# The last output stream mixed by TensorE, gelu's low part on GpSimd, and another order of units in a gated attention and stream-mixing kernel

## The chip, the cores and the metric

The kernel runs on one core of a Trainium2 chip. The metric is the device time of one execution in microseconds (us), lower is better.

## What is computed

The input x is (8, 512, 2048): eight batches of 512 rows, 2048 columns. Two blocks follow each other, each with a residual:

```
x = x + tanh(g_xattn) * xattn(layernorm(x), ctx, mask, Wq, Wk, Wv, Wo, biases)
x = x + tanh(g_ffn)   * ffn(layernorm(x), W_res, W_pre, W_post, bases, gate, W_branch)
```

xattn cuts the 2048 columns into windows of 128 and does attention inside each: q and k are projections (256 x 512) of the normalised x, v one of ctx, 8 heads of 32, the mask adds a large negative number to masked keys, and the result goes through gelu, then Wo, bias and mask. ffn sees each of the 512 rows as 4 streams of 512. From the row's logits come a 4 x 4 matrix H_res (50 Sinkhorn iterations), H_pre and H_post (softmax over 4):

```
x_pre = einsum('btnc,btn->btc', x_streams, H_pre);  y = x_pre @ W_branch
out_i = sum_j H_res[i,j] * x_j  +  H_post[i] * y          (i, j: streams)
```

## The kernel before

The program is a table of steps g, and every engine walks the same table in its own instruction order. A step with 0 <= g < 256 is a **unit**: one window of 128 columns and 4 of the 8 heads. G = g // 8 is a **chunk** (512 columns of a batch, 32 chunks), r = g % 8 the place in it. Steps from -16 to -1 are the lead-in, steps from 256 on only finish the second block.

In a step TensorE does, in this order, the scores of unit g (L688), the transposed scores of g-1 (L700, L702), values and denominators of g-2 (L715, L719), and then what `banked_at(g)` lists: projections q (r 0, 1), k (r 2, 3) and v (r 6, 7) of the next chunk, the output projection o of the chunk before (two tiles at r 4, two at r 5), transposes and logits of the chunk two before. Each such group fills one of four PSUM banks used in rotation (`RING`), and waits until the group four places earlier has been read (`bank_free`, L571). VectorE takes the row maximum (`maximum`, L998; unit g+1's scores wait for it, since there is one bank for scores), the low bf16 parts of q and k (`low_qk`), `divide` (L1005), the low part of gelu's output (`low_gelu`, L1023, r 3), `read_wo` (r 5, 6), the statistics and a mask row (`mask_row`, L991, r 4, once per chunk). ScalarE does exp, ln, gelu and the high bf16 parts; GpSimd normalises x (`norm_x`) and makes the low parts of x and ctx (`split_x`, `split_ctx`).

The second block of batch f hangs on steps 32(f+1) + e. Its Sinkhorn iterations take 26 steps (`SINK`), two iterations each, that is four halves per step: VectorE reduces and inverts (L1134, L1135), GpSimd multiplies the 4 x 4 matrices by the result (`scale`, L526), VectorE reduces the product, and so on, with other work of the step put between the halves. After that come four **tiles** of 128 rows, eight steps apart, the first at e = 52 (`TILE_AT`). With k the step counted from a tile's own:

- k = -4: ScalarE's first product of x_pre (L876); k = -3: VectorE adds three more (`make_xpre`, L1167)
- k = -1: TensorE transposes x_pre (L675), ScalarE copies it (L884); k = 0: TensorE's `branch`, 4 fp32 matmuls 128x512 (8 instructions, L728)
- k = -1 and 2: ScalarE starts the four output streams, two by two (`first_out`, L893)
- k = 0, 1, 2: VectorE adds x_1, x_2, x_3 to streams 0 and 1 (`add_stream`, L1179, two instructions a step); k = 3: adds y to all four (`add_y`, L1192); k = 4, 6, 7: x_1 to x_3 to streams 2 and 3
- GpSimd stores streams 0 and 1 at k = 4 and 2 and 3 at k = 8 (`store`, L480). The tile of the next group is started only when the pair of the tile before has been stored (`out_stored`).

SyncE issues the loads: x, ctx, masks, statistics pieces, the x1 tiles, and 12 + 12 copies per chunk that stack q and k (L390), in its own fixed order. Besides these it stores x1 (r 0) and copies the mask row under k.

Of the kernel before, what the change touches and what calls it, by code (L numbers as in the profile page):

```python
# [11 lines left out]
P = 128  # L12
B, D, S = 8, 512, 2048
W = 128
# [54 lines left out]
TILE_AT = [52 + UPC * t for t in range(DT)]  # L69
# [36 lines left out]
def stat_steps(b):  # L106

    if b == 1:
        return [1 + p for p in range(XS)]
    last = UNITS * (b - 1) + 16  # L110
    return [last - UPC * (3 - p // 4) - (p % 4 == 0) for p in range(XS)]
# [8 lines left out]
def banked_at(g):  # L120

    G, r = chunk_step(g)
    made = [("t", H, j) for H, j in at_step(g, 2, T_AT)]
    made += [("lg", H, 0) for H, j in at_step(g, 2, [LOGITS_AT])]
    made += [("sel", f, 0) for f in ffn_at(g, UPC + SELECT_AT)]
    made += [("pre", f, t) for f, t in tiles_at(g, -1)]
    if 0 <= G + 1 < NG:
        made += {0: [("q", G + 1, 0)], 1: [("q", G + 1, 1)], 2: [("k", G + 1, 0)], 3: [("k", G + 1, 1)],
                 6: [("v", G + 1, 0)], 7: [("v", G + 1, 1)]}.get(r, [])
    if 0 <= G - 1 < NG and r in (4, 5):  # L130
        made += [("o", G - 1, 2 * (r - 4)), ("o", G - 1, 2 * (r - 4) + 1)]
    if g == -1:
        made.append(("csum", 0, 0))
    return made
# [25 lines left out]
def program(nc, x, ctx4, mask_bc, mask_t, gates, wq_t, bq, wk_t, bk, wv_t, bv, wo_t, bo, wf_t, base,  # L160
            w_branch, ident, stack_i, eye4, out):
    with ExitStack() as ctx:  # L162
# [28 lines left out]
        neg_row = sb("neg_row", [1, CH], BF16)  # L191
        maskt = sb("maskt", [P, 2, S // W])
        key_bias = sb("key_bias", [P, 2, S // W])
# [52 lines left out]

        pool_ps = [ps(f"pr{i}") for i in range(RING)]
# [19 lines left out]
        maskt_loaded = [sem(f"maskt_loaded{i}") for i in range(2)]  # L267
# [52 lines left out]
        xpre_ready = sem("xpre_ready")  # L320
        y_full = sem("y_full")
# [32 lines left out]
        def _(sp):  # L354
# [10 lines left out]
            def load_maskt(b):  # L365
                sp.dma_start(maskt[:, b % 2, :], mask_t[b]).then_inc(maskt_loaded[b % 2], 16)

# [40 lines left out]
            load_maskt(0)  # L408
# [3 lines left out]
            load_maskt(1)  # L412
# [3 lines left out]
            for g in range(FIRST, LAST):  # L416
# [5 lines left out]
                if r == 0 and 0 <= G - 2 < NG:  # L422
                    store_x1(G - 2)
# [7 lines left out]
                if r == 5 and 0 <= G + 1 < NG:  # L431
                    sp.wait_ge(qk_ready, 4 * (G + 1) + 4)
                    stack(G + 1, k_st, ((k_hl, 0), (k_hl, 0), (k_hl, 1)))
                    sp.wait_ge(negrow_ready, G + 2)
                    sp.dma_start(k_st[ROWS:ROWS + 1, (G + 1) % 2].rearrange("p t h j -> p (t h) j"),
                                 bcast(neg_row[:], 1, HEADS)).then_inc(stack_loaded[(G + 1) % 2], 16)
# [7 lines left out]
                if u == UPC + 6 and g >= 0 and b + 2 < B:  # L444
                    sp.wait_ge(bias_ready, b + 1)
                    load_maskt(b + 2)

        @block.gpsimd
        def _(pool):
# [13 lines left out]
            def split_ctx(G, t):  # L463
                pool.wait_ge(ctx_hi, DT * G + t + 1)
                ins = nc.gpsimd.tensor_tensor(ctx_hl[:, 1, t, :], ctx_raw[:, t, :], ctx_hl[:, 0, t, :], ALU.subtract)  # L465
                if t == DT - 1:
                    ins.then_inc(ctx_split, 1)

# [68 lines left out]
            for g in range(FIRST, LAST):  # L537
# [20 lines left out]
                if 0 <= G - 1 < NG and r in (6, 7):  # L558
                    add_x(G - 1, r - 6)
                for done, t in tiles_at(g, 4):  # L560
                    store(done, t, 0)
                for done, t in tiles_at(g, 8):
# [5 lines left out]
        def _(pe):  # L568
            PARTS = ((0, 0), (0, 1), (1, 0))

            def bank_free(what):  # L571
# [105 lines left out]

            def scores(k):
# [53 lines left out]
            for g in range(FIRST, LAST):  # L732
# [6 lines left out]
                for what in banked_at(g):  # L739
# [13 lines left out]
                    elif what[0] == "pre":  # L753
                        transpose_pre(what)
                    else:
# [5 lines left out]
        def _(act):  # L761
# [36 lines left out]
            def exp_scores(k):  # L798
                b, w = divmod(k // ET, S // W)
                if k % UNITS == 0:  # L800
                    act.wait_ge(bias_ready, b + 1)
                act.wait_ge(st_full, k + 1)
                if k >= 2:
                    act.wait_ge(av_full, k - 1)
                nc.scalar.activation(probs[:, k % 2, :], st_ps[:], ACT.Exp,  # L805
                                     bias=key_bias[:, b % 2, w:w + 1], scale=SCALE).then_inc(exp_done, 1)
# [79 lines left out]
            def first_out(f, t, pair):  # L886
                n = DT * f + t
                if t == 0 and pair == 0:
                    act.wait_ge(coef_ready, 2 * f + 2)
                if n:  # L890
                    act.wait_ge(out_stored[pair], 16 * n)
                for i in range(2 * pair, 2 * pair + 2):
                    nc.scalar.activation(otile[:, i, :], x1t[n % 2][:, 0:C], ACT.Identity,  # L893
                                         bias=ccon[:, f % 2, t, i:i + 1],
                                         scale=cmat[:, f % 2, t, i, 0:1]).then_inc(acc_ready, 1)
# [16 lines left out]
            for g in range(FIRST, LAST):  # L912
# [8 lines left out]
                for what in banked_at(g):  # L921
# [8 lines left out]
                    elif what[0] == "pre":  # L930
                        copy_pre(what)
                for H, t in at_step(g, -1, HI_CTX_AT):
# [3 lines left out]
                if g == FIRST + UPC + 3:  # L936
# [7 lines left out]
                for done, t in tiles_at(g, -4):  # L944
                    first_products(done, t)
                for done, t in tiles_at(g, -1):
                    first_out(done, t, 0)
                for done, t in tiles_at(g, 2):
                    first_out(done, t, 1)
# [11 lines left out]
        def _(dve):  # L961
# [3 lines left out]
            def stat_piece(b, p):  # L965
                q = XS * b + p
                dve.wait_ge(xs_loaded[q % XSN], 16 * (q // XSN + 1))
                nc.vector.bn_stats(bn_a[:, p // 4, p % 4, :], xs[:, q % XSN, :]).then_inc(xs_taken, 1)
# [17 lines left out]
            def bias_row(b):  # L986
                dve.wait_ge(maskt_loaded[b % 2], 16 * (b // 2 + 1))
                nc.vector.tensor_scalar(key_bias[:, b % 2, :], maskt[:, b % 2, :], 0.0, NEG * SCALE,
                                        ALU.is_le, ALU.mult).then_inc(bias_ready, 1)

            def mask_row(G):  # L991
                dve.wait_ge(mask_loaded[G % NC], 16 * (G // NC + 1))
                if G:
                    dve.wait_ge(stack_loaded[(G - 1) % 2], STACKED * ((G - 1) // 2 + 1))
                nc.vector.tensor_scalar(neg_row[:], maskbc[0:1, G % NC, :], 0.0, NEG, ALU.is_le, ALU.mult
# [26 lines left out]

            def low_gelu(G, et):  # L1023
                n = ET * G + et
                dve.wait_ge(gelu_hi, n + 1)
                nc.vector.tensor_tensor(o_part(G, et, 1), g_sb[:, et, :], o_part(G, et, 0), ALU.subtract
                                        ).then_inc(gelu_done, 1)
# [146 lines left out]
            def add_stream(f, t, pair, j):  # L1174
                x1 = x1t[(DT * f + t) % 2]
                for i in range(2 * pair, 2 * pair + 2):
                    if j == 1 and pair == 0:
                        dve.wait_ge(acc_ready, (DT * f + t) * N + i + 1)
                    ins = nc.vector.scalar_tensor_tensor(out=otile[:, i, :], in0=x1[:, j * C:(j + 1) * C],  # L1179
                                                         scalar=cmat[:, f % 2, t, i, j:j + 1], in1=otile[:, i, :],  # L1180
                                                         op0=ALU.mult, op1=ALU.add)
                if pair and j == N - 1:
# [4 lines left out]
            def add_y(f, t):  # L1187
                dve.wait_ge(y_full, DT * f + t + 1)
                for i in range(N):
# [5 lines left out]
                    if i == 1:  # L1195
                        ins.then_inc(out_ready, 1)
# [23 lines left out]
            for g in range(FIRST, LAST):  # L1220
# [101 lines left out]
```

## Time and profile before

| | |
|---|---|
| runs | median 1905.74 us (1904.44 to 1910.57, 3 runs) |
| the profiled execution | 1909.33 us, of which the span is 1907.5 us |
| VectorE busy | 1439.4 us, 75% |
| TensorE busy (matmul) | 1392.2 us, 73% |
| ScalarE busy | 945.7 us, 50% |
| GpSimd busy | 863.2 us, 45% |
| TensorE's mean granted clock | 0.884 of full |

Times are counted from the first instruction. L numbers are lines of the kernel before. "Busy" sums instruction times; idle time is put down to what ended it. Matmuls overlap, so TensorE's busy time is somewhat above the time it really needs.

### The profile page before, as it was taken

Reading aid. Unit: us, or ns where it says so; the run is one execution under the profiler, and the core shown is the slowest. Engines: PE = TensorE matmul, PEld = TensorE weight load, DVE = VectorE, ACT = ScalarE, POOL = GpSimd, SP = SyncE. Lnnn points to the kernel's source line nnn. Section 1 sums busy time; section 2 is a strip of 40 time slices with the busy share of each in tenths; the row PEclk is TensorE's granted clock in tenths of the full one; section 3 lists DMA queues with packets and bytes.
Section 4 is the critical chain, followed back from the end, with each engine's and each line's share of the span. In section 5 each row is a group of like instructions: output and inputs, shape, how many; then the busy total and the mean of one; then the engine's idle time right before and its main releaser. Section 6 shows DMA issues by size and latency. Waiting matters only on the chain. (4 is left out here: it accounts for less than half of the span.)

```text
span 1907.5 us, 35318 instructions
## 1 busy us (share of the span) xinstructions
PE 1392.2 (73%) x12301; PEld 849.8 (45%) x12448; DVE 1439.4 (75%) x3684; ACT 945.7 (50%) x1889; POOL 863.2 (45%) x1461
## 2 busy tenths in 40 slices
PE   2788999888888787888888887878788875511323
PEld 0555556555544454445544554445455553200111
DVE  3344556767788888888888888888888888777787
ACT  2455676564655555554655555555555454210112
POOL 3433334555455545455465645554555523323310
PEclk9898999998999999998999999989999987755556
DMA  7456676566666665666666566665555543321123
GB/s 245 135 149 191 195 195 163 166 170 179 171 184 179 181 178 160 177 185 181 182 174 184 163 192 167 192 171 147 169 165 166 144 120 91 88 77 44 56 96 113
DMA packets 173984, 299.79 MB, mean 157 GB/s; under 512 B 23664, under 2 KB 74736, under 8 KB 169712
## 3 DMA queue, kind: packets, MB, share of 16 engines
q1 hardware_dynamic: 147184, 230.41, 39.2%
q0 software_dynamic: 26624, 67.12, 15.3%
q8 instruction: 100, 1.64, 0.4%
q14 instruction: 76, 0.62, 0.1%
HBM read 179.75 MB, written 67.11 MB: 129 GB/s over the span
## 5 line engine op out<-in xcount | busy, mean ns | idle before, releaser
L1134 DVE TENSOR_REDUCE ssum<-kp 128x16 f32<-128x64 f32 x768 | 181.7, 237 | 175.7 <-POOL kp L526 170.5
L526 POOL TENSOR_TENSOR kp<-ke,sv 128x64 f32<-128x64 f32 x376 | 183.9, 489 | 277.2 <-DVE sv L1135 274.4
L526 POOL TENSOR_TENSOR kp<-ke,sa 128x64 f32<-128x64 f32 x392 | 126.8, 323 | 329.1 <-DVE sa L1135 329.1
L805 ACT ACTIVATE probs<-st_ps,key_bias 128x512 f32<-128x512 f32 x256 | 174.5, 682 | 199.7 <-PE st_ps L702 193.9
L604 PE MATMUL pr<-x_hl,wk 128*128 128x512 bf16 x736 | 195.7, 422 | 66.0 <-DVE k_hl L982 65.2
L1002 DVE TENSOR_REDUCE negm<-s_ps 128x4 bf16<-128x512 f32 x256 | 167.7, 655 | 75.6 <-PE s_ps L688 73.0
L604 PE MATMUL pr<-x_hl,wq 128*128 128x512 bf16 x707 | 192.2, 420 | 44.5 <-POOL x_hl L460 38.3
L460 POOL TENSOR_TENSOR x_hl<-xc,x_hl 128x512 bf16<-128x512 f32 x128 | 157.4, 1230 | 136.9 <-ACT x_hl L773 136.5
L618 PE MATMUL pr<-wv,ctx_hl 128*128 128x256 bf16 x1536 | 188.6, 282 | 23.4 <-POOL ctx_hl L465 23.4
L465 POOL TENSOR_TENSOR ctx_hl<-ctx_raw,ctx_hl 128x512 bf16<-128x512 f32 x128 | 176.5, 1379 | 59.1 <-ACT ctx_hl L767 59.1
L688 PE MATMUL s_ps<-k_st,q_st 97*128 97x128 bf16 x1024 | 102.4, 223 | 111.4 <-DVE negm L1002 98.2
L631 PE MATMUL pr<-o_sb,wo 128*128 128x512 bf16 x714 | 176.6, 385 | 4.4 <-issue 1.5
L618 PEld LDWEIGHTS pr<-wv,ctx_hl 128*128 128x128 bf16 x1536 | 151.4, 102 | 56.7 <-issue 35.6
L688 PEld LDWEIGHTS s_ps<-k_st,q_st 97*128 97x128 bf16 x1024 | 73.6, 99 | 188.8 <-DVE negm L1002 123.0
L700 PE MATMUL st_ps<-q_st,k_st 96*128 96x128 bf16 x1024 | 149.8, 223 | 7.3 <-ACT probs L805 4.4
L604 PEld LDWEIGHTS pr<-x_hl,wk 128*128 128x128 bf16 x768 | 79.6, 106 | 160.1 <-DVE k_hl L982 64.1
L702 PE MATMUL st_ps<-id_bf,negm 128*128 128x128 bf16 x1024 | 149.3, 223 | 0.0
L1010 DVE TENSOR_TENSOR o_sb<-av_ps,rden 128x128 f32<-128x128 f32 x256 | 70.4, 275 | 104.3 <-ACT rden L814 103.9
L715 PE MATMUL av_ps<-probs,v_t 128*32 128x128 f32 x2048 | 112.2, 291 | 42.8 <-DVE o_sb L1010 42.4
L728 PE MATMUL f<-wb,xpt 128*128 128x512 f32 x256 | 135.8, 680 | 8.5 <-ACT xpt L884 8.5
L604 PEld LDWEIGHTS pr<-x_hl,wq 128*128 128x128 bf16 x768 | 76.2, 106 | 145.7 <-issue 46.9
L675 PE MATMUL pr<-id_sb,xpre 128*128 128x128 f32 x128 | 24.0, 320 | 160.2 <-DVE xpre L1167 160.2
(140 smaller groups left out, 3079.2 us busy)
## 6 DMA issues: line engine op xcount, KB each, us to landing
xs<-in_dram SPq DMA_DIRECT2D x128, 256.0 KB, 3.9
xc<-in_dram SPq DMA_DIRECT2D x32, 1024.0 KB, 5.9
ctx_raw<-in_dram SPq DMA_DIRECT2D x32, 1024.0 KB, 5.1
x1c<-in_dram POOLq DMA_DIRECT2D x64, 512.0 KB, 6.0
x_dram<-x1c SPq DMA_DIRECT2D x32, 1024.0 KB, 5.4
out_dram<-otile POOLq DMA_DIRECT2D x64, 512.0 KB, 3.5
q_st<-q_hl SPq DMA_DIRECT2D x384, 64.0 KB
k_st<-k_hl SPq DMA_DIRECT2D x384, 64.0 KB
```

Of the source, the lines that this page charges most:

```text
L460: nc.gpsimd.tensor_tensor(x_hl[:, G % 2, 1, t, :], xc[:, t, :], x_hl[:, G % 2, 0, t, :], ALU.subtract).then_inc(x_split, 1)
L465: ins = nc.gpsimd.tensor_tensor(ctx_hl[:, 1, t, :], ctx_raw[:, t, :], ctx_hl[:, 0, t, :], ALU.subtract)
L526: nc.gpsimd.tensor_tensor(kp[:], ke[:], v, ALU.mult).then_inc(kp_made, 1)
L604: ins = nc.tensor.matmul(bank(what)[:], w[:, a, t, i * P:(i + 1) * P], x_hl[:, G % 2, m, t, :], start=(t == 0 and a + m == 0), stop=(t == ...
L618: ins = nc.tensor.matmul(bank(what)[:, j * E:(j + 1) * E], ctx_hl[:, a, t, win], wv[:, m, t, :], start=(t == 0 and a + m == 0), stop=(t == ...
L631: ins = nc.tensor.matmul(bank(what)[:], wo[:, a, et, t * P:(t + 1) * P], o_part(G, et, m), start=(et == 0 and a + m == 0), stop=(et == ET ...
L688: ins = nc.tensor.matmul(s_ps[:, h * W:(h + 1) * W], q_st[0:ROWS + 1, G % 2, et, h, win], k_st[0:ROWS + 1, G % 2, et, h, win], start=True, ...
L700: nc.tensor.matmul(part, k_st[0:ROWS, G % 2, et, h, win], q_st[0:ROWS, G % 2, et, h, win], start=True, stop=False)
L702: ins = nc.tensor.matmul(part, negm[:, k % 2, h:h + 1].broadcast_to([P, P]), id_bf[:], start=False, stop=True)
L805: nc.scalar.activation(probs[:, k % 2, :], st_ps[:], ACT.Exp, bias=key_bias[:, b % 2, w:w + 1], scale=SCALE).then_inc(exp_done, 1)
L1002: nc.vector.tensor_reduce(negm[:, k % 2, :], s_ps[:].rearrange("p (h j) -> p h j", h=HPT), AX.X, ALU.max, negate=True).then_inc(max_done, 1)
L1134: cf.link(nc.vector.tensor_reduce(s_t, k, AX.X, ALU.add))
```

## The change

1. **The last stream goes to TensorE.** Stream 3 of a tile is sum_j H[3,j] x_j. GpSimd makes four 128x128 diagonal matrices from the coefficients (`make_diag`, k = -1); TensorE multiplies them with the x1 tile, 4 fp32 matmuls 128x512 into one bank (`mix`, k = 1, behind `branch`); ScalarE writes the bank out with its constant (`copy_mix`, k = 1) in place of its `first_out` for that stream. VectorE's three additions for it go. Stream 2 keeps its three on VectorE, now one behind the other at k = 5.
2. **low_gelu moves from VectorE (r 3) to GpSimd (r 4)**, between parts 0 and 1 of `scale`; `make_diag` stands between parts 2 and 3.
3. **Mask rows and key biases are made once**, in the lead-in, from two loads, in place of one VectorE instruction per chunk and one per batch.
4. **Another order.** Both v groups at r 4 (were r 6, 7), o at r 5 and 6 (were 4, 5), transposes, logits, splits and statistics at other r; tiles start at e = 54; inside a tile: x_pre at k = -2, streams 0 and 1 at k = 1, 3, 4, y at k = 2, stores at k = 5 and 6; add_x h = 1 at r 0 of the next chunk, the x1 store at r 2, the ctx load at r 4.

```diff
-NORM_AT, HI_X_AT, LOW_X_AT = [2, 3, 4, 5], [3, 4, 5, 6], [4, 5, 6, 7]
-HI_CTX_AT, LOW_CTX_AT = [0, 0, 1, 4], [1, 2, 3, 5]
-T_AT, LOGITS_AT, SELECT_AT = [2, 2, 3, 3], 4, 6
-STAT_B_AT = [2, 4]
+NORM_AT, HI_X_AT, LOW_X_AT = [2, 3, 4, 5], [3, 5, 5, 6], [5, 6, 6, 7]
+HI_CTX_AT, LOW_CTX_AT = [-1, 0, 0, 1], [0, 1, 2, 3]
+T_AT, LOGITS_AT, SELECT_AT = [3, 4, 4, 5], 6, 7
+STAT_B_AT = [2, 5]
-TILE_AT = [52 + UPC * t for t in range(DT)]
+TILE_AT = [54 + UPC * t for t in range(DT)]
-    return [last - UPC * (3 - p // 4) - (p % 4 == 0) for p in range(XS)]
+    return [UNITS * (b - 1) + UPC * (p // 4 - 2) + (1, 5, 6, 6)[p % 4] for p in range(XS)]
@@ banked_at @@
+    made += [("mix", f, t) for f, t in tiles_at(g, 1)]
-                 6: [("v", G + 1, 0)], 7: [("v", G + 1, 1)]}.get(r, [])
-    if 0 <= G - 1 < NG and r in (4, 5):
+                 4: [("v", G + 1, 0), ("v", G + 1, 1)]}.get(r, [])
+    if 0 <= G - 1 < NG and r in (5, 6):
@@ sync @@
-            load_maskt(0)
+            sp.dma_start(maskt, mask_t.rearrange("b p n -> p b n")).then_inc(masks_loaded, 16)
+            sp.dma_start(mask_rows, mask_bc.rearrange("b (n j) -> (b n) j", j=CH)).then_inc(masks_loaded, 16)
-                if r == 0 and 0 <= G - 2 < NG:
+                if r == 2 and 0 <= G - 2 < NG:
                     store_x1(G - 2)
-                if r == 6 and 1 <= G + 2 < NG:
+                if r == 4 and 1 <= G + 2 < NG:
                     sp.wait_ge(ctx_split, G + 2)
                     load_ctx(G + 2)
@@ gpsimd @@
+            def low_gelu(G, et):
+                pool.wait_ge(gelu_hi, ET * G + et + 1)
+                nc.gpsimd.tensor_tensor(o_part(G, et, 1), g_sb[:, et, :], o_part(G, et, 0), ALU.subtract
+                                        ).then_inc(gelu_done, 1)
+            def make_diag(f, t):
+                ...
+                for j in range(N):
+                    ins = nc.gpsimd.tensor_scalar(diag[:, j, :], id_sb[:], cmat[:, f % 2, t, N - 1, j:j + 1], None,
+                                                  ALU.mult)
+                ins.then_inc(diag_made, 1)
+                if 0 <= G - 1 < NG and r == 4:
+                    for et in range(ET):
+                        low_gelu(G - 1, et)
+                for ready, t in tiles_at(g, -1):
+                    make_diag(ready, t)
@@ tensor @@
+                elif kind == "mix":
+                    pe.wait_ge(acc_ready, N * (DT * c + i) + 3)
+            def mix(what):
+                ...
+                pe.wait_ge(diag_made, n + 1)
+                for j in range(N):
+                    ins = nc.tensor.matmul(bank(what)[:], diag[:, j, :], x1t[n % 2][:, j * C:(j + 1) * C],
+                                           start=(j == 0), stop=(j == N - 1))
+                ins.then_inc(bank_full, 1)
@@ scalar @@
+            def copy_mix(what):
+                ...
+                act.wait_ge(bank_full, PLACE[what] + 1)
+                if n:
+                    act.wait_ge(out_stored[1], 16 * n)
+                nc.scalar.activation(otile[:, N - 1, :], bank(what)[:], ACT.Identity,
+                                     bias=ccon[:, f % 2, t, N - 1:N]).then_inc(acc_ready, 1)
@@ vector @@
-                if 0 <= G - 1 < NG and r == 3:
-                    for et in range(ET):
-                        low_gelu(G - 1, et)
-                for k, pair, j in ((0, 0, 1), (1, 0, 2), (2, 0, 3), (4, 1, 1), (6, 1, 2), (7, 1, 3)):
+                for k, j in ((1, 1), (3, 2), (4, 3)):
                     for done, t in tiles_at(g, k):
-                        add_stream(done, t, pair, j)
-                for done, t in tiles_at(g, 3):
+                        add_stream(done, t, j, (0, 1))
+                for done, t in tiles_at(g, 2):
                     add_y(done, t)
-                for done, t in tiles_at(g, -3):
+                for done, t in tiles_at(g, 5):
+                    for j in range(1, N):
+                        add_stream(done, t, j, (2,))
+                for done, t in tiles_at(g, -2):
                     make_xpre(done, t)
-                if r == 0 and 0 <= G + 1 < NG and (G + 1) % NC == 0:
-                    bias_row((G + 1) // NC)
-                if r == 4 and 0 <= G + 1 < NG:
-                    mask_row(G + 1)
+                if g == -6:
+                    mask_parts()
```

## Rows read from the trace of the kernel before

**Rows 1.** The page: the span and the engines' busy time, share and instructions

```profile
span 1907.5 us, 35318 instructions
...
PE 1392.2 (73%) x12301; PEld 849.8 (45%) x12448; DVE 1439.4 (75%) x3684; ACT 945.7 (50%) x1889; POOL 863.2 (45%) x1461
```

**Rows 2.** Windows: length, busy PE, PEld, DVE, ACT, POOL (count), clock, DMA share, GB/s

```profile
70.00:388.00 318.00, 280.63 (x2862) 178.95 (x2892) 172.76 (x399) 186.79 (x388) 131.94 (x182) 0.96 0.62 173
...
788.00:1412.00 624.00, 512.01 (x4596) 311.40 (x4656) 529.88 (x1372) 350.83 (x705) 330.55 (x546) 0.94 0.61 174
...
1600.00:1830.00 230.00, 62.74 (x218) 32.52 (x216) 171.52 (x501) 41.74 (x76) 73.19 (x186) 0.58 0.23 73
```

**Rows 3.** Groups by line in 788 to 1412 us: count | busy us, mean ns | idle before

```profile
L1002 DVE TENSOR_REDUCE negm<-s_ps 128x4 bf16<-128x512 f32 x96 | 62.2, 648 | 2.6 <-PE s_ps L688 2.4
```

**Rows 4.** VectorE's waits in 788 to 1412 us: total us, times, longest us

```profile
DVE ssum L1134 <- POOL kp L526: 52.0, 80, 1.6
DVE o_sb L1010 <- ACT rden L814: 21.5, 19, 1.8
```

**Rows 5.** TensorE's waits in 788 to 1412 us

```profile
PE s_ps L688 <- DVE negm L1002: 47.7, 42, 3.0
PE pr L604 <- DVE k_hl L982: 37.6, 12, 3.7
```

**Rows 6.** Timeline of VectorE in one chunk: start, us, instructions, idle before

```profile
904.10 2.32 DVE L1167 SCALAR_TENSOR_TENSOR xpre<-x1t_even,pre,xpre 128x512 f32<-128x512 f32 x3
...
916.17 1.29 DVE L1026 TENSOR_TENSOR o_sb<-g_sb,o_sb 128x512 bf16<-128x512 f32 x2 [0.23 <-ACT o_sb L830]
917.38 1.41 DVE L1179 SCALAR_TENSOR_TENSOR otile<-x1t_odd,cmat,otile 128x512 f32<-128x512 f32 x2
```

**Rows 7.** Groups by line, whole span

```profile
L454 POOL TENSOR_SCALAR xc<-xc,ra 128x512 f32<-128x512 f32 x128 | 106.9, 835 | 9.0 <-DMA xc<-in_dram 7.5 <-POOL ra L500 1.4
...
L787 ACT ACTIVATE q_hl<-pr,bq_sb 128x512 bf16<-128x512 f32 x64 | 43.9, 685 | 140.9 <-PE pr L604 140.9
...
L995 DVE TENSOR_SCALAR neg_row<-maskbc 1x512 bf16<-1x512 f32 x32 | 17.9, 561 | 0.4 <-issue 0.2
...
L507 POOL TENSOR_SCALAR rb<-mv_b 128x4 f32<-128x4 f32 x8 | 1.9, 232 | 0.7
```

**Rows 8.** The instructions of line 460: shortest/median/longest ns

```profile
L460 POOL TENSOR_TENSOR x_hl<-xc,x_hl x128: 1145/1159/2054, 30.9 to 1512.8; 128x512 bf16<-128x512 f32 x128
```

**Rows 9.** Timeline of TensorE in one chunk

```profile
921.95 3.60 PE L728 MATMUL f<-wb,xpt 128*128 128x512 f32 x8
...
931.65 2.78 PE L618 MATMUL pr<-wv,ctx_hl 128*128 128x256 bf16 x24 [0.88 <-POOL ctx_hl L465]
```

**Rows 10.** Timeline of TensorE in the lead-in

```profile
58.67 7.68 PE L618 MATMUL pr<-wv,ctx_hl 128*128 128x256 bf16 x48 [8.26 <-POOL ctx_hl L465]
```

**Rows 11.** The chain that ended last, in the last Sinkhorn steps: start, us

```profile
1706.15 0.30 POOL kp L526
...
1707.02 1.29 DVE otile L1179 x2
```

**Rows 12.** The same chain, last four tiles

```profile
1840.25 7.03 DMA out_dram<-otile
...
1857.15 6.94 DMA out_dram<-otile
...
1864.83 0.81 ACT otile L893
...
1889.56 5.36 PE f L728 x8
...
1895.02 2.74 DVE otile L1192 x4
```

**Rows 13.** Timeline of TensorE, last four tiles

```profile
1839.09 6.68 PE L728 MATMUL f<-wb,xpt 128*128 128x512 f32 x8 [0.69 <-ACT xpt L884]
...
1887.79 1.09 PE L675 MATMUL pr<-id_sb,xpre 128*128 128x128 f32 x4 [9.79 <-DVE xpre L1167]
```

More of the change, by code:

```diff
@@ L266, in program @@
         mask_loaded = [sem(f"mask_loaded{i}") for i in range(NC)]
-        maskt_loaded = [sem(f"maskt_loaded{i}") for i in range(2)]
+        masks_loaded = sem("masks_loaded")
         stack_loaded = [sem(f"stack_loaded{i}") for i in range(2)]
@@ L754, in _ @@
                         transpose_pre(what)
+                    elif what[0] == "mix":
+                        mix(what)
                     else:
@@ L884, in copy_pre, with first_out @@
                 nc.scalar.activation(xpt[:], bank(what)[:], ACT.Copy).then_inc(xt_copied, 1)
-            def first_out(f, t, pair):
+            def first_out(f, t, i):
                 n = DT * f + t
-                if t == 0 and pair == 0:
+                if t == 0 and i == 0:
                     act.wait_ge(coef_ready, 2 * f + 2)
-                if n:
[L891 to L895, printed above, removed]
+                if n and i != 1:
+                    act.wait_ge(out_stored[i // 2], 16 * n)
+                nc.scalar.activation(otile[:, i, :], x1t[n % 2][:, 0:C], ACT.Identity,
+                                     bias=ccon[:, f % 2, t, i:i + 1],
+                                     scale=cmat[:, f % 2, t, i, 0:1]).then_inc(acc_ready, 1)
+            def copy_mix(what):
+                kind, f, t = what
+                n = DT * f + t
+                act.wait_ge(bank_full, PLACE[what] + 1)
+                if n:
+                    act.wait_ge(out_stored[1], 16 * n)
+                nc.scalar.activation(otile[:, N - 1, :], bank(what)[:], ACT.Identity,
+                                     bias=ccon[:, f % 2, t, N - 1:N]).then_inc(acc_ready, 1)
             def w_parts(i, dst, loaded):
@@ L931, in _ @@
                         copy_pre(what)
+                    elif what[0] == "mix":
+                        copy_mix(what)
                 for H, t in at_step(g, -1, HI_CTX_AT):
@@ L943, in _ @@
                     xstat(b + 1)
-                for done, t in tiles_at(g, -4):
+                for done, t in tiles_at(g, -5):
                     first_products(done, t)
[L946 to L949, printed above, removed]
+                for done, t in tiles_at(g, 0):
+                    for i in range(2):
+                        first_out(done, t, i)
+                for done, t in tiles_at(g, 1):
+                    first_out(done, t, 2)
                 for n in range(2):
@@ L967, in stat_piece @@
                 dve.wait_ge(xs_loaded[q % XSN], 16 * (q // XSN + 1))
+                if b and p == 0:
+                    dve.wait_ge(mv_a_ready, b)
                 nc.vector.bn_stats(bn_a[:, p // 4, p % 4, :], xs[:, q % XSN, :]).then_inc(xs_taken, 1)
@@ L1172, in make_xpre, with add_stream @@
                 ins.then_inc(xpre_ready, 1)
[L1174 to L1179, printed above, removed]
+            def add_stream(f, t, j, which):
+                n = DT * f + t
+                for i in which:
+                    if j == 1 and i < 2:
+                        dve.wait_ge(acc_ready, N * n + i + 1)
+                    ins = nc.vector.scalar_tensor_tensor(out=otile[:, i, :], in0=x1t[n % 2][:, j * C:(j + 1) * C],
                                                          scalar=cmat[:, f % 2, t, i, j:j + 1], in1=otile[:, i, :],
                                                          op0=ALU.mult, op1=ALU.add)
-                if pair and j == N - 1:
+                if j == N - 1:
                     ins.then_inc(out_ready, 1)
```

71 lines of the change are left out of this document (33 added, 38 removed).

## The prediction

> **What bounds the kernel now.** I read the page first, for the share of each engine, then windows by stage, then the waits inside the longest stage, and last the chain that ended last. The sum is made against the profiled execution, 1909.3 us with a span of 1907.5 [rows 1]; the median of the runs shown is 3.6 us lower, and I subtract that at the end. About 0.3% (5.7 us) is what a measurement of this kernel can tell from no change.
>
> Four stages need different readings. From 70 to 388 us (the first 64 units) TensorE is busy 281 of 318 us and VectorE only 173 [rows 2]: TensorE sets the pace. From 788 to 1412 us VectorE takes its maximum 96 times [rows 3], so these 624 us are 12 chunks of 52.0 us. VectorE is busy 529.9 us of them, 44.2 per chunk [rows 2]; for the rest it waits 52.0 us for GpSimd's Sinkhorn products and 21.5 for ScalarE's reciprocals, and for TensorE's scores only 2.4 [rows 3, 4]. TensorE waits 47.7 us there for VectorE's maximum and 37.6 for its low_qk [rows 5]. So VectorE's own list, with the Sinkhorn waits in it, is the pace. From 1600 us to the end there are no units. Until about 1830 the chain is the Sinkhorn alternation with tile work between the halves [rows 11]; then come four tiles, 16.9 us apart, each with a 7 us store in its chain (two stores start at 1840.25 and 1857.15) [rows 12].
>
> **The tile stage: units 84 to 256, 21.5 chunks.** VectorE loses per chunk:
> - three additions of stream 3: a pair takes 1.41 us [rows 6], so 2.1 us;
> - two low_gelu: 1.29 us and a wait of 0.23 in front [rows 6], 1.5 us;
> - one mask row, 0.56 us in the mean [rows 7].
>
> That is 4.2 us of 52.0. What comes back:
> - Stream 2's three additions now follow each other, each waiting for the one before. The dependent three of x_pre take 2.32 us against 2.1 for interleaved ones [rows 6]: +0.2.
> - Sinkhorn waits. Each half needs GpSimd's product, and an addition between two halves hides it. Before, six steps of a tile held a pair between halves, now three hold a pair and one all of stream 2. GpSimd gets 2 low_gelu, priced by its subtraction of the same shape, 1.16 us each [rows 8], between parts 0 and 1 of r 4: 2.3 us where one split_x of 1.16 stood. VectorE reaches that half about 2 us into the unit (maximum, half, low_qk, divide), so about 1 us shows. The two split_x at r 6 lie behind read_wo and show less. The four diagonals of 128 columns are bounded by 0.23 us (4 columns) and 0.84 (512 columns) [rows 7]; between them by width it is about 0.4 each, 1.5 us a tile, under the statistics of r 5. The waits are 4.3 us a chunk now [rows 4]; I take +1.0, between 0 and +3.
> - TensorE gets `mix`, of branch's shape and count, 3.6 us [rows 9]. Its busy time per chunk goes from 42.7 [rows 2] to 46.3. It has 9.3 us of idle time, but the new order makes lumps: at r 4 both v groups (2.8 us each [rows 9]) and two transposes, of which the second v must wait for the bank of k 1, which VectorE's low_qk frees in the same unit; at r 6 two o, logits and branch, with the last o behind read_wo. VectorE's lead of one unit absorbs the first; at r 7 its maximum comes up short by something from 0 to 2.5 us. I take +0.5.
>
> ScalarE swaps a first_out of 0.81 us [rows 12] for a copy of a bank with a bias, 0.69 [rows 7], and is half idle: nothing. SP's moved issues (x1 store, ctx load, add_x) each keep at least a unit before their reader: nothing, and if that cover fails a chunk starts some us late.
>
> Net 4.2 - 0.2 - 1.0 - 0.5 = 2.5 us per chunk, between 0.5 and 4.0; times 21.5 = **-54 us** (-11 to -86).
>
> A rule weighed. low_gelu costs GpSimd 1.16 us by the row, against 0.65 on VectorE (1.29 for two) [rows 6, 8], 1.8 times.
> The Trainium skill (GPSIMD Reference, Engine selection) advises against elementwise work with two inputs on GpSimd, which it calls about twice slower than VectorE; by that factor the pair would take 0.3 us more per chunk, an estimate of 6 us over the stage.
> The sum goes by the row.
>
> **Before the tiles (70 to about 500 us, 10.5 chunks).** TensorE does the same work but r 7 now holds only its attention part, which is too short to cover the round from scores to maximum and back, and r 3 has less work under ScalarE's gelu block. I take +0.8 us a chunk over 8 chunks, less 2 or 3 us where Sinkhorn already runs and VectorE is relieved: **+4 us** (-5 to +10).
>
> **Lead-in.** TensorE stands 8.26 us for the last part of ctx in front of v [rows 10]. The splits of ctx and Wv come earlier, but k's stacks follow the same clock: **-3 us** (-6 to +3, since the mask load of all batches now lies in front of ctx).
>
> **Sinkhorn steps after the last unit (1600 to 1830).** An inserted pair adds 1.29 us and hides a product of 0.30 and two handovers, 0.4 in all [rows 11], so 0.9 net. Per tile before: six pairs; now three pairs and one group of three (2.3 - 0.4). That is 5.3 against 4.6, and low_gelu goes once: **-4 us** for four tiles (-8 to +4, since y now has only four steps for branch and mix at a low clock).
>
> **The last four tiles.** Before, branch ran beside VectorE's additions and the store was the chain. Now, from x_pre ready: transposes 1.09 [rows 13], handovers and copy 0.8, branch 5.36 [rows 12], then mix behind it on the same engine, then copy_mix 0.69, first_out 0.81, half of add_y 1.4, two pairs 2.8, stream 2 2.3, the next x_pre 2.3. Branch took 5.36 to 6.68 here [rows 12, 13] and 3.6 in the busy stage [rows 9], where the granted clock is 0.94 and not 0.58 [rows 2]. Since mix follows without a pause on an engine that has just worked 5 us, I take 4.4, between 3.6 and 6.7. The period is then 22.0 us, against 16.9: three periods +15. The last tile has the same +5, and before the first x_pre VectorE now has two pairs and stream 2 more but one pair less: +4. Together **+25 us**, between +14 (both matmul groups at 3.6) and +39 (both at 6.7). The store leaves the chain: it has 13 us beside the next branch and mix.
>
> Sum: -54 + 4 - 3 - 4 + 25 = -32 us: 1909.3 - 32 = 1877, and 3.6 less for the median: about 1874 us.
>
> **Rivals.**
> - **A, TensorE becomes the pace (slower).** For: 46.3 us busy per chunk leaves 5.7 us for waits if the chunk is to be shorter than 52. Today's idle is 9.3, 4.0 of it for the maximum (that vanishes if TensorE is late) and 3.1 for low_qk [rows 5]. If the low_qk wait moves to the second v at r 4 and the r 6 lump adds 2 us, the chunk is about 52.5. It decides from 5.7 us of such waits on. Against: VectorE waits for scores only 0.2 us per chunk now. Price: +0.5 x 21.5 = +11, and the other terms +22: 1939 us. Chance 0.15.
> - **B, GpSimd's list becomes the Sinkhorn chain.** For: its subtraction takes up to 2.05 us where the median is 1.16 [rows 8]. The waits then grow by 3 us per chunk and the gain is 0.5: 1909.3 - 11 + 22 - 3.6 = 1917, or 1908 where they grow by 2.6. The Trainium skill (SBUF — State Buffer, Who interferes with whom) has the shared port pair of VectorE and GpSimd as an exclusive lock; the long instances would agree with it, the median, close to the shortest, does not. Chance 0.12.
> - **C, the cover was better than I think.** 4.0 us a chunk is kept, the early stage costs nothing, the last tiles cost +18: 1909.3 - 86 - 3 - 4 + 18 - 3.6 = 1831. For: the new order spreads VectorE's list evenly, and its longest units (r 4 and r 7) lose most. Chance 0.15.
> - **D, the stage is worth no more than the end costs.** Gain of 1 us per chunk, -21 against +25: no change. It would mean that ScalarE's reciprocals, 1.8 us per chunk now [rows 4], or a DMA take the place of the removed work. Chance 0.08.
>
> **Numbers.** My forecast has 0.50: 1874 us, with its own range 1850 to 1900. The range 1838 to 1915 leaves out A and most of C's and B's outer halves. Faster by over 0.3%: nearly all of the forecast and C, a little of B and D, 0.69. Within 0.3%: half of B and of D, 0.10. Slower: A and the rest, 0.21.
>
> **What would show it.** Right: in the tile stage a chunk of 49 to 50 us, VectorE busy about 40 of it, its Sinkhorn waits near 5 us, its wait for scores under 1; GpSimd busy near 980 us in all; TensorE near 1520; the last four tiles 21 to 23 us apart with branch and mix in the chain and no store. Wrong: VectorE waiting for scores at r 6 to r 0 by over 2 us per chunk (A), Sinkhorn waits over 7 us (B), stores still in the last tiles' chain, or a tile period under 19 us.

## The result, and the profile after

The changed kernel took 1915.72 us in the median of 8 runs (1908.43 to 1918.80), the kernel before 1904.64 (8 runs): a ratio of 1.0047, 95% interval 1.0029 to 1.0064. It is **slower by half a per cent**. I had forecast 1874 us, faster by 1.6%. The profiled execution after took 1918.8 us with a span of 1917.0; it is the slowest of the eight, and two of them took 1908.4 and 1909.4.

First the page of the changed kernel, the answer to [rows 1].

```profile
span 1917.0 us, 35771 instructions
...
PE 1458.7 (76%) x12548; PEld 880.6 (46%) x12704; DVE 1346.0 (70%) x3486; ACT 943.2 (49%) x1889; POOL 995.8 (52%) x1653
```

VectorE did lose work, 93 us of it, and GpSimd gained 133. The engine that set the pace got lighter, and the time went up. TensorE gained only 66.5 us, though `mix` (L709) is busy for 125.6: its other matmuls got shorter (those of q and k, L630, took 392 and 386 ns in the mean, against 420 and 422 before). The prediction had TensorE near 1520.

The windows by stage, as in [rows 2] (length, busy time of PE, PEld, DVE, ACT, POOL, granted clock, DMA share, GB/s):

```profile
70.00:388.00 318.00, 274.50 (x2824) 178.51 (x2860) 158.00 (x359) 187.68 (x385) 141.09 (x186) 0.95 0.64 172
...
788.00:1412.00 624.00, 544.34 (x4785) 328.19 (x4845) 504.14 (x1313) 357.37 (x720) 387.69 (x628) 0.98 0.62 177
1600.00:1830.00 230.00, 81.54 (x227) 39.88 (x227) 161.11 (x465) 34.48 (x65) 83.66 (x206) 0.64 0.23 74
1830.00:1917.00 87.00, 39.90 (x76) 17.07 (x76) 43.59 (x61) 15.44 (x23) 13.60 (x21) 0.72 0.23 84
```

To see where the time went I took the start of every maximum of VectorE (one per unit) and of the transposes of x_pre (one group per tile) from the two timelines:

| stretch | before | after | difference | forecast |
|---|---|---|---|---|
| start to unit 0 | 70.1 | 70.2 | 0 | -3 |
| units 0 to 63 | 318.0 | 321.8 | +4 | +4 |
| units 64 to 255 | 1214.1 | 1189.5 | -25 | -54 |
| last unit to the first of the last four tiles | 235.2 | 247.2 | +12 | 0 |
| last four tiles to the end | 70.2 | 88.4 | +18 | +21 |

(The forecast's +4 for VectorE's reordered work ahead of the first x_pre belongs to the fourth line, next to the -4 of the Sinkhorn steps.) Two lines are wrong: the tile stage gave 25 us and not 54, and the Sinkhorn steps after the last unit cost 12.

One line that agrees does so by luck. Unit 64 begins at 392.0 us in this trace. In the traces of x1, x3, x4, z1 and w3 below it begins at 381.0 to 385.9, and their edits touch only what comes later (the first diagonal is made at 499.7 us). Their units 0 to 63 take 314.5 to 317.1 us, where the changed kernel took 321.8 and the kernel before 318.0. So some 6 to 11 us of this profiled span come from no part of the change that was varied here. What they are, and how many of the other seven runs have them, stays open, and the half per cent of the result (11 us) is of the same size. Differences between traces are therefore given by stage from here on.

VectorE's and TensorE's waits in the same 624 us as [rows 4, 5] (total us, times, longest):

```profile
DVE ssum L1173 <- POOL kp L543: 64.9, 123, 1.2
DVE negm L1047 <- PE s_ps L723: 26.0, 17, 3.6
DVE o_sb L1055 <- ACT rden L851: 12.5, 15, 2.4
```

```profile
PE s_ps L723 <- DVE negm L1047: 21.3, 35, 1.3
PE av_ps L750 <- DVE o_sb L1055: 17.9, 28, 1.4
PE pr L657 <- DVE x1c L1064: 14.7, 9, 2.5
```

The chunk is 51.1 us (three batches, units 128 to 223, in 613 us) against 52.0. Per chunk of 51.1 VectorE is busy 41.3 (44.2 before), waits 5.3 for Sinkhorn products (4.3), 2.1 for scores (0.2) and 1.0 for reciprocals (1.8). A new line stands among TensorE's waits: an output projection (L657) that waits for VectorE to read an earlier one. Of what the prediction named as signs, the wait for scores of over 2 us per chunk (rival A) is there; Sinkhorn waits over 7 (rival B) are not.

After the last unit there is a new entry in the chain that ended last; part of that chain:

```profile
1728.86 2.33 POOL diag L482 x4
...
1764.61 2.32 POOL diag L482 x4
...
1804.41 2.32 POOL diag L482 x4
```

And the last four tiles, the chain of the first of them, the answer to [rows 12]:

```profile
1828.64 1.10 PE pr L701 x4
...
1830.42 5.78 PE f L763 x8
1836.19 3.45 PE pr L709 x8
...
1840.25 0.81 ACT otile L929
...
1841.09 1.42 DVE otile L1231 x2
1842.53 1.43 DVE otile L1218 x2
1843.98 2.09 DVE otile L1218 x3
```

mix (L709) stands behind branch (L763) in the chain, no store is in it, and the tiles are 21.4, 20.9 and 20.7 us apart, where they were 16.9.

### The profile page after: what moved, and what is told of

Read it like the earlier page. It is cut to its first block and busy times, and to the rows that moved or that the text cites. A ratio compares the mean times of both kernels' runs of the same rounds, so it can differ in the third digit from the quotient of the medians.

```text
span 1917.0 us, 35771 instructions
## 1 busy us (share of the span) xinstructions
PE 1458.7 (76%) x12548; PEld 880.6 (46%) x12704; DVE 1346.0 (70%) x3486; ACT 943.2 (49%) x1889; POOL 995.8 (52%) x1653
## 5 line engine op out<-in xcount | busy, mean ns | idle before, releaser
L842 ACT ACTIVATE probs<-st_ps,key_bias 128x512 f32<-128x512 f32 x256 | 174.2, 681 | 226.6 <-PE st_ps L737 224.1
L543 POOL TENSOR_TENSOR kp<-ke,sv 128x64 f32<-128x64 f32 x376 | 166.7, 443 | 222.9 <-DVE sv L1174 219.5
L543 POOL TENSOR_TENSOR kp<-ke,sa 128x64 f32<-128x64 f32 x392 | 116.3, 297 | 298.0 <-DVE sa L1174 298.0
L630 PE MATMUL pr<-x_hl,wq 128*128 128x512 bf16 x707 | 175.3, 392 | 44.8 <-POOL x_hl L459 37.7
L644 PE MATMUL pr<-wv,ctx_hl 128*128 128x256 bf16 x1536 | 176.4, 273 | 33.6 <-DVE k_hl L1032 20.2
L657 PE MATMUL pr<-o_sb,wo 128*128 128x512 bf16 x705 | 175.0, 386 | 29.9 <-DVE x1c L1064 26.2
L464 POOL TENSOR_TENSOR ctx_hl<-ctx_raw,ctx_hl 128x512 bf16<-128x512 f32 x128 | 165.4, 1296 | 59.3 <-ACT ctx_hl L804 59.3
L459 POOL TENSOR_TENSOR x_hl<-xc,x_hl 128x512 bf16<-128x512 f32 x128 | 148.0, 1168 | 57.0 <-ACT x_hl L810 56.8
L630 PE MATMUL pr<-x_hl,wk 128*128 128x512 bf16 x736 | 173.7, 386 | 2.1 <-issue 0.5
L644 PEld LDWEIGHTS pr<-wv,ctx_hl 128*128 128x128 bf16 x1536 | 147.5, 98 | 59.0 <-DVE k_hl L1032 25.8
L763 PE MATMUL f<-wb,xpt 128*128 128x512 f32 x256 | 136.3, 682 | 5.5 <-ACT xpt L921 5.5
L657 PEld LDWEIGHTS pr<-o_sb,wo 128*128 128x128 bf16 x768 | 71.9, 99 | 135.7 <-DVE x1c L1064 35.2
L630 PEld LDWEIGHTS pr<-x_hl,wq 128*128 128x128 bf16 x768 | 72.1, 100 | 132.2 <-POOL x_hl L459 37.1
```

The lines of the kernel that those rows point to most:

```text
L543: nc.gpsimd.tensor_tensor(kp[:], ke[:], v, ALU.mult).then_inc(kp_made, 1)
L630: ins = nc.tensor.matmul(bank(what)[:], w[:, a, t, i * P:(i + 1) * P], x_hl[:, G % 2, m, t, :], start=(t == 0 and a + m == 0), stop=(t == ...
L644: ins = nc.tensor.matmul(bank(what)[:, j * E:(j + 1) * E], ctx_hl[:, a, t, win], wv[:, m, t, :], start=(t == 0 and a + m == 0), stop=(t == ...
L657: ins = nc.tensor.matmul(bank(what)[:], wo[:, a, et, t * P:(t + 1) * P], o_part(G, et, m), start=(et == 0 and a + m == 0), stop=(et == ET ...
L763: ins = nc.tensor.matmul(f1[:], xpt[:, j * P:(j + 1) * P], wb[:, j, :], start=(j == 0), stop=(j == C // P - 1))
```

## The experiments

Two theories. **Theory 1**: mix, the diagonals and low_gelu give back on GpSimd and TensorE what they free on VectorE. **Theory 2**: the parts are good, and the new order of units is what costs. All ratios are to the kernel before, run on the same chip beside each group of kernels.

### Parts of the change taken back

```diff
 x1_nomix: the changed kernel, stream 3 on VectorE
-    made += [("mix", f, t) for f, t in tiles_at(g, 1)]
-                for ready, t in tiles_at(g, -1):
-                    make_diag(ready, t)
-                    first_out(done, t, 2)
+                    for i in (2, 3):
+                        first_out(done, t, i)
-                        add_stream(done, t, j, (2,))
+                        add_stream(done, t, j, (2, 3))
```

> The changed kernel with stream 3 back on VectorE beside stream 2 (k = 5), no diagonals and no mix. Theory 1 (mix and its diagonals give back what they free): per chunk VectorE gets 2.1 us more work, loses about 2 us of waits for scores and 0.8 of Sinkhorn waits, so the tile stage stays as it is, the end too (period of the last tiles 20 against 20.8 us): 1905 to 1915 us, no slower than the changed kernel. Theory 2 (the new order of units is what costs, mix itself is a gain): 2.1 us more per chunk, 45 us in all: about 1950 us.

Measured: 1969.17 us, ratio 1.0323 (1.0300 to 1.0347). 2.7% above the changed kernel, some 53 us. My theory 1 said no slower, and fell in this form: in the new order mix does relieve VectorE, by 54 us in units 64 to 255, where I had 45 us for its additions. With three additions more in one step, r 3 grows from 6.3 to 9.6 us.

```diff
 x2_gelu_dve: the changed kernel, low_gelu on VectorE at r 3
 (gpsimd)
-                if 0 <= G - 1 < NG and r == 4:
-                    for et in range(ET):
-                        low_gelu(G - 1, et)
 (vector, ahead of half_at(f, its, 1))
+                if 0 <= G - 1 < NG and r == 3:
+                    for et in range(ET):
+                        low_gelu(G - 1, et)
```

> The changed kernel with low_gelu back on VectorE at r 3. If GpSimd's part of it is what delays the Sinkhorn products (theory 3): faster than the changed kernel by 5 to 15 us. If the move is a gain of its own: VectorE has 1.4 us more per chunk and saves at most 1 us of wait, 5 to 20 us slower.

Measured: 1918.73 us, ratio 1.0064 (1.0041 to 1.0086), which overlaps the interval of the changed kernel. By the medians the move of low_gelu is worth nothing that I could tell from zero. The trace is of the slowest of five runs (1940.54 us, 22 above the median) and can't price it; its Sinkhorn waits are 56.0 us in the 624 against 64.9, as VectorE's work comes back. That is 9 of the 13 us by which these waits grew over the kernel before.

```diff
 x12_order_only: both of these edits together
```

> The changed kernel without mix and with low_gelu on VectorE: the new order and the masks alone, with the additions to streams 2 and 3 together at k = 5 as in x1 (1969 us). If low_gelu's move is worth little with the additions on VectorE too: 1965 to 1985 us. Against the kernel before (1907) this says what the new order costs without the relief that it was made for: about 60 us.

Measured: 1960.57 us, ratio 1.0278 (1.0244 to 1.0312). The new order with the masks alone is 2.8% slower than the kernel before; it needs mix. This kernel also has the lump at k = 5, so it does not price the order by itself.

### The parts in the old order

y1 is the kernel before with the change's `mix`, `make_diag` and `copy_mix`, y2 the kernel before with its low_gelu on GpSimd, y3 both with `mask_parts`:

```diff
 y1_before_mix
+    made += [("mix", f, t) for f, t in tiles_at(g, 2)]
-                for i in range(2 * pair, 2 * pair + 2):
+                for i in range(2 * pair, min(2 * pair + 2, N - 1)):
+                for ready, t in tiles_at(g, -1):
+                    make_diag(ready, t)
```

> The kernel before with stream 3 on TensorE alone (diagonals by GpSimd at k = -1, mix at k = 2 behind branch, copy at k = 2). Putting stream 3 back on VectorE cost the changed kernel 54 us. If mix is worth that much in itself, this is 1865 to 1880 us, and the new order is what takes the gain away. If it is worth it only where stream 3 would have made a lump at k = 5, this is 1895 to 1915 us: 1 us per chunk gained, 10 us lost at the end.

Measured: 1923.13 us, ratio 1.0079 (1.0060 to 1.0097).

> The kernel before with low_gelu on GpSimd at r 3. In the changed kernel the move was worth 0.3% (putting it back cost 3 us against the median there). Here GpSimd's 2.4 us stand in front of part 1 at r 3 and o follows at r 4: a gain of 1.4 us per chunk less 1 to 2 us of waits: 1895 to 1920 us.

Measured: 1920.11 us, ratio 1.0058 (1.0036 to 1.0080).

> The kernel before with mix, low_gelu on GpSimd (r 3) and the masks made once, all in the old order of units. Theory 2 (the order costs): well under the changed kernel, 1860 to 1885 us. Theory 1 (the parts themselves give back what they free): within 10 us of the changed kernel, 1905 to 1925.

Measured: 1927.82 us, ratio 1.0098 (1.0073 to 1.0123). Theory 2 wanted 1860 to 1885 and falls: in the old order the same three parts are worse than in the new one by half a per cent. VectorE's waits in the same 624 us show the return. y1, y2 and y3 in turn, each against 52.0 us in [rows 4]:

```profile
DVE ssum L1175 <- POOL kp L541: 74.3, 98, 3.2
```

```profile
DVE ssum L1136 <- POOL kp L531: 67.7, 88, 2.8
```

```profile
DVE ssum L1168 <- POOL kp L542: 93.2, 109, 3.2
```

mix alone adds 22 us of Sinkhorn waits, low_gelu alone 16, both (with the masks) 41. VectorE's busy time in the window falls by 30, 16 and 45. What is taken from VectorE and given to GpSimd comes back as a wait for GpSimd.

### The diagonals

```diff
 x3_diag_act: the changed kernel, diagonals by ScalarE (k = -1)
-                    ins = nc.gpsimd.tensor_scalar(diag[:, j, :], id_sb[:], cmat[:, f % 2, t, N - 1, j:j + 1], None,
-                                                  ALU.mult)
+                    ins = nc.scalar.activation(diag[:, j, :], id_sb[:], ACT.Copy,
+                                               scale=cmat[:, f % 2, t, N - 1, j:j + 1])
```

> The changed kernel with the diagonals made by ScalarE (4 activations of 128 columns a tile) and not by GpSimd. Theory 1: GpSimd's 2.33 us per tile stand between two Sinkhorn products; gone, the waits for products fall by about 0.8 us per chunk and by 1.9 us per tile after the last unit: 15 to 25 us faster than the changed kernel. Theory 2: no difference beyond 5 us.

Measured: 1898.21 us, ratio 0.9952 (0.9934 to 0.9970): 17 us under the changed kernel and now faster than before. Of the 21.6 us between the two profiled spans, 8.7 lie before unit 64, where neither kernel has made a diagonal. 6.7 lie in units 64 to 255 and 6.4 in the Sinkhorn steps after them: the traces give the diagonals 13 us, and only 0.3 per tile in the tile stage. VectorE's Sinkhorn waits in the 624 us hardly change (64.9 before this edit):

```profile
DVE ssum L1185 <- POOL kp L543: 63.3, 116, 1.2
```

One of GpSimd's diagonals took 592 ns, one of ScalarE's 394.

```diff
 w3_double_diag: the changed kernel, each diagonal also into an unread tile
+                for j in range(N):
+                    nc.gpsimd.tensor_scalar(diag2[:, j, :], id_sb[:], cmat[:, f % 2, t, N - 1, j:j + 1], None,
+                                            ALU.mult)
```

> The changed kernel with GpSimd making each diagonal twice, the first time into a tile that nobody reads. Moving them away gained 17 us. If GpSimd's list is in series with the Sinkhorn halves, a further 2.33 us per tile cost at least as much again: 32 tiles x 2.33 = 75 us at most, 25 to 60 expected, 1940 to 1975. If GpSimd has slack there, under 10 us.

Measured: 1974.72 us, ratio 1.0356 (1.0341 to 1.0372), 59 us above the changed kernel, of 75 us that were added to GpSimd. By the traces, units 64 to 255 take 57 us longer (2.6 for each of the 22 tiles in them) and the Sinkhorn steps after them 12. GpSimd is half idle by the page, and at this place it had room for the first set (0.3 us per tile, x3) and none for a second.

```diff
 w2_before_mix_act: y1 with the diagonals by ScalarE (k = 0)
```

> The kernel before with mix alone, as y1, but the diagonals made by ScalarE (k = 0). y1 was 1923 us, 14.5 above the kernel before. If GpSimd's diagonals between the Sinkhorn products are what cost: 15 to 25 us less than y1, 1898 to 1908. If the cost of mix in the old order is TensorE's: within 5 us of y1.

Measured: 1908.44 us, ratio 1.0012 (0.9994 to 1.0030) against 1.0079 for y1: 13 us of y1's 15 were the diagonals. The traces place the gain: 8.7 us in the Sinkhorn steps after the last unit (235.2 to 226.6), and only 1.3 in units 64 to 255. There the wait for products falls from 74.3 to 49.8 us, but the one for reciprocals rises from 22.5 to 40.3: ScalarE, which now makes the diagonals, is waited for instead.

### TensorE's place for mix and for the logits

```diff
 x4_mix_early: the changed kernel, mix ahead of the transposes of x_pre
-    made += [("mix", f, t) for f, t in tiles_at(g, 1)]
+    made += [("mix", f, t) for f, t in tiles_at(g, -1)]     (listed ahead of "pre")
 copy_mix at k = 0, make_diag at k = -3, mix also waits for x1t_loaded
```

> The changed kernel with mix ahead of the transposes of x_pre (k = -1), its copy at k = 0 and the diagonals at k = -3. Theory 1: mix leaves the chain of the last four tiles, which gives 3.4 us for mix and 1 to 1.5 for its copy each, about 18 us, and the lump of r 6 and r 7 is taken apart, up to 1 us per chunk: 1880 to 1900 us. Theory 2: the last tiles alone, 18 us, units unchanged.

Measured: 1992.37 us, ratio 1.0444 (1.0423 to 1.0464). A clear miss: the last tiles are 18.3 us apart as hoped, but in the units TensorE has v twice at r 4, then mix, transposes and two o at r 5, then branch at r 6. VectorE's wait for scores goes from 26.0 to 80.5 us in the 624:

```profile
DVE negm L1048 <- PE s_ps L724: 80.5, 25, 4.9
```

So the early place is right only where no units run:

```diff
 z1_hybrid: x3_diag_act, and for the last batch x4's order
+    made += [("mix", f, t) for f, t in tiles_at(g, -1) if f == B - 1]
     made += [("pre", f, t) for f, t in tiles_at(g, -1)]
+    made += [("mix", f, t) for f, t in tiles_at(g, 1) if f < B - 1]
```

> The changed kernel with the diagonals on ScalarE, and for the last batch's four tiles mix ahead of the transposes of x_pre, its copy at k = 0. Diagonals on ScalarE alone gave 1898 us. In the kernel with mix early everywhere the last tiles were 18.3 us apart against 20.9: here 3 us for each of the four, about 1886 to 1890 us. If it is no faster than 1898, the period of the last tiles is set by something else than mix in the chain.

Measured: 1886.65 us, ratio 0.9883 (0.9862 to 0.9903). The last tiles are 17.9, 18.1 and 18.3 us apart, where x3's were 20.8, 22.4 and 21.4.

```diff
 w4_best_gelu_dve: z1_hybrid with x2's edit
```

> The hybrid (1887 us) with low_gelu back on VectorE at r 3. 1.4 us more per chunk on VectorE, Sinkhorn waits less by up to 1 us: 3 to 12 us slower, 1890 to 1899. If GpSimd is the tighter of the two, faster than 1884.

Measured: 1897.75 us, ratio 0.9948 (0.9932 to 0.9965). With the diagonals away from GpSimd, low_gelu's move is worth 11 us (7 to 17 by the intervals of the ratios); beside them it was worth 3 (-2 to 9). These overlap, so that the two moves hinder each other isn't shown.

```diff
 v1_after_lg7: the changed kernel; w5_best_lg7: z1_hybrid
-T_AT, LOGITS_AT, SELECT_AT = [3, 4, 4, 5], 6, 7
+T_AT, LOGITS_AT, SELECT_AT = [3, 4, 4, 5], 7, 8
```

> The changed kernel with the logits' matmuls at r 7 and select one step later, nothing else. In the hybrid this gave 22 us. If TensorE's lump at r 6 is a cost of its own, the same here: 1890 to 1898 us. If it only counts once GpSimd's diagonals are gone, under 10 us: 1906 to 1914.

> The hybrid with the logits' matmuls at r 7 and not r 6 (select one step later). At r 6 TensorE has logits, two o and branch and VectorE waits about 1 us for its scores there and at r 7. If the lump makes the wait, it shrinks by 0.5 to 1 us per chunk, 10 to 20 us: 1867 to 1877. If the wait is only passed on to r 7, where mix stands, no change.

Measured: v1 1891.11 us, ratio 0.9924 (0.9894 to 0.9954), 24 us under the changed kernel by one line (in the traces 17.5 of it in units 64 to 255, and 9.0 before unit 64, where x3 without this edit is as fast); w5 **1864.53 us, ratio 0.9776 (0.9756 to 0.9796)**, the fastest of all, 40 us under the kernel before. VectorE's waits of v1 in the same window:

```profile
DVE ssum L1173 <- POOL kp L543: 72.7, 133, 1.6
DVE o_sb L1055 <- ACT rden L851: 11.0, 19, 1.0
DVE negm L1047 <- PE s_ps L723: 8.1, 6, 2.5
```

The wait for scores falls from 26.0 to 8.1 us, r 6 gets shorter by 1.0 us in the mean, r 0 by 0.5 and r 7 by 0.3, and TensorE's wait of 14.7 us for x1c is gone from its list:

```profile
PE s_ps L723 <- DVE negm L1047: 24.7, 31, 2.4
PE pr L644 <- DVE k_hl L1032: 14.2, 13, 1.6
PE av_ps L750 <- DVE o_sb L1055: 11.1, 20, 1.4
```

Two things move, and no run takes them apart. The logits' 1.0 us leaves the step with two o and branch. And the four banks are used in rotation: with the logits in front, the last o took the bank that the first o had filled, which VectorE reads in that same step; without them it takes the bank of the x_pre transposes, which ScalarE has long copied.

TensorE at r 6 and r 7 in v1 (timeline):

```profile
1003.88 2.76 PE L657 MATMUL pr<-o_sb,wo 128*128 128x512 bf16 x12
1006.49 3.60 PE L763 MATMUL f<-wb,xpt 128*128 128x512 f32 x8
...
1011.16 1.04 PE L684 MATMUL pr<-xt,wf 128*32 128x512 f32 x8
1012.13 3.70 PE L709 MATMUL pr<-x1t_even,diag 128*128 128x512 f32 x8
```

The second o and branch follow each other with no gap. In the changed kernel the last o stood, and VectorE's maximum after it came late; the timelines of TensorE and of VectorE there:

```profile
1020.28 1.47 PE L657 MATMUL pr<-o_sb,wo 128*128 128x512 bf16 x6 [0.57 <-DVE x1c L1064]
1021.58 3.60 PE L763 MATMUL f<-wb,xpt 128*128 128x512 f32 x8
```

```profile
1025.44 0.69 DVE L1047 TENSOR_REDUCE negm<-s_ps 128x4 bf16<-128x512 f32 x1 [0.82 <-PE s_ps L723]
```

## Why the prediction was wrong

The reading of the kernel before held: VectorE's list with the Sinkhorn waits in it set the pace, TensorE the first 64 units, the store the last four tiles. The direction failed on sizes, and most of the misses point the same way.

- **Tile stage, net 2.5 us per chunk: it was 0.9 in the 12 chunks read.** Term by term: VectorE's busy time fell by 2.9 and not by 4.0. The Sinkhorn waits rose by 1.0, as said, and mostly from low_gelu, as said: without its move they are 8.9 us lower in the 624 (x2; 11.4 from z1 to w4), without GpSimd's diagonals 1.6 (x3). The diagonals were mis-sized (592 ns each, against 0.4), but here they did lie almost wholly under other work. The wait for scores rose by 1.9, not 0.5. That is **the step that failed most**: I named the lump at r 6 "with the last o behind read_wo" and the range of 0 to 2.5 us, and took a value near its lower end, because VectorE's lead of one unit would absorb it. v1, which takes the logits out of r 6, brings this wait from 2.1 to 0.6 us per chunk and the run down by 24 us (17.5 in this stage). Reciprocals gave 0.8 back, where I had nothing.
- **VectorE's busy time.** Three additions a tile went, but the 288 that stay got longer: 235.3 us, where 384 took 267.1. The longest takes 2.67 us against 1.28 before. With low_gelu off GpSimd (x2) the ones on the odd tile fall from 911 ns in the mean to 789, and the even ones stay at 780. The changed kernel, then x2:

```profile
L1218 DVE SCALAR_TENSOR_TENSOR otile<-x1t_odd,cmat,otile 128x512 f32<-128x512 f32 x144 | 127.0, 911 | 6.9 <-ACT otile L929 5.2
```

```profile
L1221 DVE SCALAR_TENSOR_TENSOR otile<-x1t_odd,cmat,otile 128x512 f32<-128x512 f32 x144 | 109.4, 789 | 6.9 <-ACT otile L926 5.2
```

The same edit made on z1 (w4) takes them from 907 to 788. So 17.6 us of low_gelu's move came back on VectorE by itself. I had no term for it, though rival B had the same cause on the other engine. Before, the two groups took 745 and 729 ns; the rest of the lengthening was not taken apart.

- **Sinkhorn steps after the last unit, 0 with the +4 of the reordered work: it was +12.** The diagonals have nothing to lie under here. At three tiles VectorE waits 2.08 us for the product behind them, where it otherwise waits 0.41: 5 us, and x3 wins 6.4 there. The runs take the rest apart as well. This stretch took 235.2 us before, 253.6 and 253.1 with the new order and stream 3 on VectorE (x1, x12), 240.8 with mix and ScalarE's diagonals (x3), 247.2 with GpSimd's. So the new order (with three more additions at k = 5) costs 18, mix gives back 12 to 13, and GpSimd's diagonals take 6. One part of the order I overlooked: the Sinkhorn iterations start one step later, and 156 products in place of 153 come after the last unit.
- **Last four tiles, +21: it was +18**, the mechanism as told: mix behind branch in the chain, the store out of it. mix took 3.45, just under the lower bound of 3.6, and branch 5.1 to 6.7. x4 and z1 confirm the chain by moving mix out of it. (The prediction's parts for the end add up to 24 and not 25.)
- **First 64 units +4: +4, by luck.** Five kernels with the same list there took 1 to 3.5 us less than the kernel before. **Lead-in -3: 0** in this trace, and -1 to -4 in those five.
- **low_gelu's move.** I counted 1.5 us per chunk for it. In the changed kernel it is worth nothing measurable (x2), in the old order it costs 11 us (y2), in z1 it is worth 11 (w4). What it is worth depends on the order around it.
- **Rivals.** A said that TensorE's lumps would make it slower, with the place right (r 6, wait for low_qk at the second v) and a price of 1939; its sign showed, its price did not. B said that GpSimd's list would become the Sinkhorn chain; that held after the last unit and hardly in the tile stage. I weighed them as alternatives, but their costs are paid together: 17 (x3) + 24 (v1) + 12 (x3 to z1) = 53 us by the medians, which from 1916 gives 1863. w5, with all three repairs, ran 1864.5. In the traces w5 is 55.2 us shorter than the changed kernel, of which 8.8 lie before unit 64 and belong to the open difference there; 29.4 lie in units 64 to 255, 6.3 in the Sinkhorn steps and 10.8 in the last four tiles.

With the three places repaired the change is thus worth 40 us. How much of it is mix, low_gelu, the masks or the repaired order itself is not shown: no run has w5's order without the parts.

## What to carry to other kernels

Work taken from the engine that sets the pace is gained only if its new engine is not one that the pace-setter waits for just then: price a move by what stands behind it on the new engine's queue, not by that engine's idle share. A doubled copy of the suspect shows whether there is room for more, not what the first copy costs: for that, take it away, and read both runs by stage. With banks in rotation, ask for each group which reader frees its bank; moving a group by one place changes the reader of all that follow. Where a kernel has a stretch without its main work, give that stretch its own order, since an engine that hides an operation in one stage puts it in the chain of the other.

## What the runs showed of the hardware that I had not expected

- A diagonal (128x128 fp32, one input and a scalar per partition) took GpSimd 592 ns in the median and 648 in the mean, where 128x512 with two operations took 835 in the mean and 4 columns 232 [rows 7]: far from proportional to the columns. ScalarE took 394 ns for it (median).
- Additions on VectorE with two inputs in SBUF are at times stretched beside GpSimd's subtraction: up to 2.67 us against a median of 0.75 (1.72 at most in x2), and the mean of one group falls by 13% when low_gelu leaves GpSimd. The Trainium skill (SBUF — State Buffer, Who interferes with whom) has these two engines share a port pair under an exclusive lock; the stretched additions agree with it, though I did not isolate a pair. The two engines at one such place in the changed kernel, VectorE first:

```profile
904.35 3.88 DVE L1218 SCALAR_TENSOR_TENSOR otile<-x1t_odd,cmat,otile 128x512 f32<-128x512 f32 x3
```

```profile
904.46 1.66 POOL L470 TENSOR_TENSOR o_sb<-g_sb,o_sb 128x512 bf16<-128x512 f32 x1 [2.71 <-ACT o_sb L867]
```

At 952.80 three such additions took 3.01 us beside another subtraction of GpSimd's, the split of ctx (L464); with no such subtraction beside them, at 1717.54, they took 2.1.

- The granted clock of TensorE in the tile stage rose from 0.94 to 0.98. The extra matmuls alone do not do it (y1, mix in the old order: 0.94), nor does the new order alone (x12: 0.95); both together reach 0.96 (x2) to 0.99 (v1).
